# Macaron block on one core: all nine second products of a group as split products, and a ninth low half made on GpSimd

## Chip, core and metric

The kernel runs on one NeuronCore of a Trainium2 chip. The metric is the device time of one execution in microseconds (us). Times are the median of three executions. All inputs and outputs are float32. The engines are called PE (TensorE), DVE (VectorE), ACT (ScalarE), POOL (GpSimd) and SP (SyncE, which here only issues DMAs).

## What is computed

```python
x = x + 0.5 * ffn(layernorm(x))        # x: 8 x 1024 x 128
x = x + attention(layernorm(x))        # causal, one head, width 128
x = x + 0.5 * ffn(layernorm(x))

def ffn(h):                            # h: tokens x 128
    cw = route(sigmoid(h @ Wg.T))      # 16 experts, 4 chosen per token, weights
    hid = relu(h @ W1[e].T) ** 2       # 64 wide per expert
    y = hid @ W2[e].T
    return sum_e(cw[e] * y[e]) + relu(h @ Ws1.T) ** 2 @ Ws2.T
```

## The kernel before

The 8192 tokens are cut into 64 tiles of 128 and 16 groups of four tiles (512 tokens). A feed-forward phase runs over the 16 groups, then attention runs over eight batches, then a second feed-forward phase runs over the same groups. That is 32 groups in all. Everything in a group is transposed: features lie on partitions, tokens on the free axis, so a PE product has 512 columns.

All 16 experts are computed for every token. Two experts of 64 make one chunk of 128 hidden features, eight chunks hold the experts and a ninth (index 8) the shared expert. So `NCH` is 9, and a group has nine first products (`up`) and nine second products (`down`), which add up in one PSUM bank.

Float32 accuracy comes from splitting. An operand is stored as a high half, rounded to the type fp32r, and a low half, the rest. `split3` (L1186) makes one product out of three fp32r matmuls: high by high, high by low, low by high. One of the second products, chunk 5 (`WHOLE = (5,)`, L121), is different: it is one plain float32 matmul on unsplit operands (L1249), which the profile shows as two passes.

For chunk m the work goes through the engines in this order:
- PE: `up` (L1237), three matmuls into one of three PSUM banks (`HB`).
- DVE: `gate` (L931), relu times the routing weight out of `wb` into `s_sb` (L939; L941 for the shared chunk).
- ACT: `square` (L499), the square of `s_sb` twice, once rounded into `g_hi` (L504, left out for chunk 5) and once in full into `g_f` (L505). The second one counts up `sq_done`.
- POOL: `lo_part` (L374), `g_lo = g_f - g_hi` (L379), which counts up `glo_done`. For chunk 5 it returns at once.
- PE: `down` (L1244). It waits for `glo_done`, or for `sq_done` where the chunk is 5.

In the trace `g_f` is called `shared`, and `g_hi` and `g_lo` are both called `shared_r`.

The order on each engine is written out by hand, and each engine runs its list in order. The bodies are L1314 (PE), L1013 (DVE), L557 (ACT) and L418 (POOL); two groups make one pass of the loop. The up product, gate, square and low half of a chunk stand `AHEAD` = 4 chunks ahead of its down product, and `s_sb`, `g_f`, `g_hi` and `g_lo` are rings of six. In between, every group also has on PE the router's product (L1227) and three sets of transposes (L1219, L1235, L1261); on DVE the routing (`route`, parts 0 to 9) and layer norm statistics; on ACT four normalisations (L460) and several copies; on POOL one power operation for both inverse roots, `inv_and_norm_root` (L391, the instruction is L398), and the low half of the next input, `x_lo_part` (L382, L385).

Where they stand on POOL within a group: low half of chunk 4, then at place c = 1 the power operation, which waits among others for `wsum_done` of DVE (L919); then the low halves of chunks 6, 7, 8 and of the next group's chunk 0; then `x_lo_part`; then the next group's 1, 2, 3 and 4. On DVE at place c = 0 stands route part 7, which ends with L914 (`chosen`, from two operands in SBUF); at c = 1 the gate of chunk 5 and route part 8, which ends with L919; at c = 2 the gate of chunk 6.

The routing weights of a group come as a broadcast over DMA: ACT copies them (`wT_copy`), SP stores them to DRAM and loads them spread over the partitions into `wb` (L318).

At the end of the first phase the attention's opening is woven into the last group (`begin`, L623 on ACT and L1098 on DVE): after the square of chunk 5 ACT copies `z_hi` (L593), and DVE makes `z_lo` from it (L1059) between the gates of chunks 6 and 7.

Of the kernel before, what the change touches and what calls it, by code (L numbers as in the profile page):

```python
# [26 lines left out]
ACT = mybir.ActivationFunctionType  # L27
AX = mybir.AxisListType

P = 128  # L30
# [73 lines left out]
def macaron_kernel(nc, x, Qw, Kw, Vw, Wg, bias_corr, W1, W2, Ws1, Ws2, out):  # L104
    B, S, D = x.shape
# [5 lines left out]
    F = E * I + Ws1.shape[0]  # L111
    NCH = F // P
# [5 lines left out]
    HB = 3  # L118
    RING = 6

    WHOLE = (5,)  # L121
    PREP = 4
    PR = 4
    PADT = 3 * TG
# [8 lines left out]
    with ExitStack() as ctx:  # L133
        def sb(name, shape, dt=F32):
            return ctx.enter_context(nc.sbuf_tensor(name, shape, dt))
# [12 lines left out]
        w1_lo = sb("w1_lo", [P, NCH, P], F32R)  # L148
        w2_hi = sb("w2_hi", [P, NCH, D], F32R)
        w2_lo = sb("w2_lo", [P, NCH, D], F32R)  # L150
        w2_f = sb("w2_f", [P, len(WHOLE), D])
        wgT = sb("wgT", [P, E])
        qkT = sb("qkT", [P, 2, P])
        m_hi = sb("m_hi", [P, P], F32R)
# [43 lines left out]
        s_sb = sb("s_sb", [P, RING, GT])  # L198
# [3 lines left out]
        g_f = shared[:, 0:RING * GT].rearrange("p (r n) -> p r n", r=RING)  # L202
        g_hi = shared_r[:, 0:RING * GT].rearrange("p (r n) -> p r n", r=RING)
# [22 lines left out]
        o_ps = [psum[:, 3, :], psum[:, 4, :]]  # L226
# [116 lines left out]
        @block.gpsimd  # L343
        def _(pool):
            nc.gpsimd.memset(ident[:], 0.0).then_inc(self_done, 1)
            nc.gpsimd.memset(maskb[:], 0.0).then_inc(self_done, 1)
            nc.gpsimd.memset(neg_half[:], -0.5).then_inc(const_done, 1)
            pool.wait_ge(self_done, 2)
            nc.gpsimd.affine_select(out=ident[:], in_=ident[:], compare_op=ALU.not_equal, fill=1.0, base=0,
                                    pattern=[[-1, P]], channel_multiplier=1).then_inc(const_done, 1)  # L350

            nc.gpsimd.affine_select(out=maskb[:], in_=maskb[:], compare_op=ALU.is_ge, fill=MASKED, base=0,
                                    pattern=[[-1, P]], channel_multiplier=1).then_inc(const_done, 1)

            nc.gpsimd.memset(x_sb[:, NT:NT + PADT, :], 0.0).then_inc(const_done, 1)

            def inv_std(S_, n, var, out_, readers):

                pool.wait_ge(S_.var_done, n + 1)
                for r, count in readers:  # L360
                    wait(pool, r, count)
                nc.gpsimd.tensor_tensor(out_, var, neg_half[:, 0:out_.shape[1]], ALU.pow).then_inc(S_.rstd_done, 1)  # L362

            def attention_inv(b):
                inv_std(AT, b, a_mv[:, :, 1], a_rstd[:], [(AT.zn_done, 2 * b)])

            def ffn(F):
                def norm_root(g):

                    pool.wait_ge(F.wsum_done, g + 1)  # L370
                    wait(pool, F.scw_done, g)
                    nc.gpsimd.tensor_tensor(wroot, wsum, neg_half[:, 0:TG], ALU.pow).then_inc(F.norm_done, 1)

                def lo_part(m, j):  # L374

                    if j % NCH in WHOLE:
                        return
                    pool.wait_ge(F.sq_done, m + 1)
                    nc.gpsimd.tensor_tensor(g_lo[:, j % RING, :], g_f[:, j % RING, :], g_hi[:, j % RING, :].bitcast(F32),  # L379
                                            ALU.subtract).then_inc(F.glo_done, 1)  # L380

                def x_lo_part(g, u):  # L382

                    pool.wait_ge(F.xhi_done, g + 1)
                    nc.gpsimd.tensor_tensor(x_lo[:, u, :], x_f[:, u, :], x_hi[:, u, :].bitcast(F32),  # L385
                                            ALU.subtract).then_inc(F.xlo_done, 1)

                def inv(n):
                    inv_std(F, n, var, rstd, [(F.xn_done, n), (F.xn2_done, n)])

                def inv_and_norm_root(g):  # L391

                    pool.wait_ge(F.var_done, g + PREP + 1)
                    pool.wait_ge(F.wsum_done, g + 3)
                    pool.wait_ge(F.xn_done, g + PREP)
                    pool.wait_ge(F.xn2_done, g + PREP)
                    pool.wait_ge(F.scw_done, g + 2)
                    nc.gpsimd.tensor_tensor(roots[:], powers[:], neg_half[:, 0:2 * TG], ALU.pow).then_inc(F.rstd_done, 1)  # L398

                def start():  # L400
                    inv(0)
                    inv(1)
                    if F is FF[0]:
                        x_lo_part(0, 0)
                        norm_root(0)
                        inv(2)
                    else:
                        attention_inv(B - 1)
                        inv(2)
                        x_lo_part(0, 0)  # L410
                        norm_root(0)
                    x_lo_part(1, 1)
                    inv(3)
                    norm_root(1)
                    for m in range(AHEAD):
                        lo_part(m, m)

                def body(i, last):  # L418
                    for u in range(UN):
                        g = i * UN + u  # L420
                        for c in range(NCH):
                            j = u * NCH + c
                            if c == 1 and not last:
                                inv_and_norm_root(g)
                            if c == 6 and not last:
                                x_lo_part(g + 2, u)
                            if last and F is FF[0] and j == 4:
                                attention_inv(0)
                            if not (last and j + AHEAD >= UN * NCH):
                                lo_part(i * (UN * NCH) + j + AHEAD, (j + AHEAD) % (UN * NCH))  # L430

                start()
                body(0, False)
                with pool.Fori(1, NG // UN - 1) as i:
                    body(i, False)
                body(NG // UN - 1, True)

            ffn(FF[0])
            with pool.Fori(1, B - 1) as b:
                attention_inv(b)  # L440
            ffn(FF[1])
# [3 lines left out]
        def _(sc):  # L445
            copy = lambda o, i, scale=1.0: nc.scalar.activation(o, i, ACT.Copy, scale=scale)  # L446
# [20 lines left out]
            def ffn(F, phase):  # L467
# [31 lines left out]
                def square(m, j):  # L499

                    sc.wait_ge(F.s_done, m + 1)
                    wait(sc, F.down_done, m + 1 - RING)
                    if j % NCH not in WHOLE:
                        nc.scalar.activation(g_hi[:, j % RING, :], s_sb[:, j % RING, :], ACT.Square)  # L504
                    nc.scalar.activation(g_f[:, j % RING, :], s_sb[:, j % RING, :], ACT.Square).then_inc(F.sq_done, 1)  # L505

                def first_half(n):
# [46 lines left out]
                def lead(c):  # L554
                    square(c, c)
# [122 lines left out]
            def weights_hi(w):  # L678

                sc.wait_ge(wt_done, w + 1)  # L680
                src = wt_ps[w]
                flat = lambda a, k: a[:, 4 * k:4 * k + 4, :].rearrange("p c n -> p (c n)")
                if w < 2:
                    copy(flat(w1_hi, w), src).then_inc(wt_hi, 1)
                elif w < 4:
                    for n, c in enumerate(WHOLE):
                        if c // 4 == w - 2:
                            copy(w2_f[:, n, :], src[:, (c % 4) * P:(c % 4 + 1) * P])
                    copy(flat(w2_hi, w - 2), src).then_inc(wt_hi, 1)
                else:  # L690
                    copy(w1_hi[:, NC, :], src[:, 0:P])
                    copy(w2_hi[:, NC, :], src[:, P:2 * P])
                    copy(qkT[:].rearrange("p c n -> p (c n)"), src[:, 2 * P:4 * P]).then_inc(wt_hi, 1)
# [489 lines left out]
        def _(pe):  # L1183
            mm = nc.tensor.matmul
# [29 lines left out]
            def ffn(F, phase):  # L1214
# [29 lines left out]
                def down(g, c, m, j, u):  # L1244
                    if c == 0:
                        wait(pe, F.oT_copied, g - 1)
                    if c in WHOLE:
                        pe.wait_ge(F.sq_done, m + 1)
                        mm(o_ps[u], w2_f[:, WHOLE.index(c), :], g_f[:, j % RING, :], start=(c == 0),  # L1249
                           stop=(c == NCH - 1)).then_inc(F.down_done, 1)  # L1250
                        return
                    pe.wait_ge(F.glo_done, g * (NCH - len(WHOLE)) + sum(k not in WHOLE for k in range(c + 1)))
                    split3(o_ps[u], w2_hi[:, c, :], w2_lo[:, c, :], g_hi[:, j % RING, :], g_lo[:, j % RING, :],
                           start=(c == 0), stop=(c == NCH - 1)).then_inc(F.down_done, 1)

# [268 lines left out]
```

## Time and profile before

| | |
|---|---|
| median of 3 executions | 702.88 us (702.61 to 703.27) |
| the profiled execution's own time | 702.95 us |
| its span, first to last instruction | 701.2 us |
| PE busy | 673.3 us (96%) |
| DVE busy | 567.5 us (81%) |
| ACT busy | 529.6 us (76%) |
| POOL busy | 438.2 us (62%) |
| first feed-forward phase | about 33 to 268 us |
| attention | about 268 to 466 us |
| second feed-forward phase | about 466 to 701 us |

Busy shares are means over stages: POOL has next to nothing to do in attention, so its 62% says little of its load in the two other phases. The granted PE clock is at its full level (2.4 GHz, shown as 1.0) in the whole span. Matmul ends in the records are modelled, so the distance from one start to the next tells more of what a matmul costs than its duration.

### The profile page before, as it was taken

To read this page: it belongs to the slowest core of one execution; us is meant where nothing else is said; L and a number is where in the kernel's file an instruction comes from. 1 tells how busy PE (TensorE), PEld (TensorE's weight loads), DVE (VectorE), ACT (ScalarE), POOL (GpSimd) and SP (SyncE) were. 2 spreads that over 40 slices of the span, in tenths; PEclk is the share of its full clock that TensorE was granted. 3 is DMA by queue.
4 is the path that set the end of the run, shared out by engine and by line. 5 is a ranking of instruction groups with operands and counts; after the bars stand their busy time and mean duration, and the time that the engine had idled before them with its cause. 6 is when DMAs were issued, how large, how long until landed. Compare 5 with 4: busy or idle time off the path is not lost.

```text
span 701.2 us, 15091 instructions
## 1 busy us (share of the span) xinstructions
PE 673.3 (96%) x3367; PEld 527.5 (75%) x3367; DVE 567.5 (81%) x2586; ACT 529.6 (76%) x1094; POOL 438.2 (62%) x346
## 2 busy tenths in 40 slices
PE   4799999999999997999999999999999999999997
PEld 4567878888788875787778777778788887888775
DVE  5898998899888985666656678898988998889863
ACT  3578888888888866675566477659888788887875
POOL 3379888998889972000000021148889898898875
PEclk9999999999999999999999999999999999999999
DMA  9856776567765640000000000365776787767782
GB/s 246 196 124 138 162 165 145 124 147 154 162 143 123 152 90 0 1 1 1 0 1 0 0 0 1 71 134 115 158 166 140 166 179 171 165 139 174 166 178 72
DMA packets 53525, 78.37 MB, mean 112 GB/s; under 512 B 5216, under 2 KB 19184, under 8 KB 53488
## 3 DMA queue, kind: packets, MB, share of 16 engines
q1 hardware_dynamic: 51280, 77.36, 50.4%
q10 hardware_dynamic: 2208, 0.59, 0.4%
q8 instruction: 14, 0.23, 0.1%
q14 instruction: 23, 0.19, 0.1%
HBM read 72.70 MB, written 5.24 MB: 111 GB/s over the span
## 4 chain that ended last, share of the span: by engine, by line
PE 78%; DVE 10%; ACT 5%; issue 3%; POOL 1%; DMA 1%; POOLq 0%; DVEq 0%; ACTq 0%
PE psum L1188 18%; PE psum L1190 18%; PE psum L1189 18%; PE psum L1397 7%; PE psum L1227 4%; PE psum L1249 4%; DVE nmax L1068 3%; PE psum L1219 2%; PE psum L1261 2%; PE psum L1386 2%; ACT shared L611 2%; PE psum L1410 2%; DVE zn L1082 1%; DVE s_sb L939 1%; ACT wb L446 1%
## 5 line engine op out<-in xcount | busy, mean ns | idle before, releaser
L379 POOL TENSOR_TENSOR shared_r<-shared,shared_r 128x512 fp32r<-128x512 f32 x256 | 325.9, 1294 | 55.6 <-ACT shared L505 53.5
L939 DVE SCALAR_TENSOR_TENSOR s_sb<-psum,wb 128x512 f32<-128x512 f32 x256 | 175.5, 687 | 46.2 <-PE psum L1190 25.9
L505 ACT ACTIVATE shared<-s_sb 128x512 f32<-128x512 f32 x288 | 178.1, 620 | 28.6 <-DVE s_sb L939 28.6
L504 ACT ACTIVATE shared_r<-s_sb 128x512 fp32r<-128x512 f32 x256 | 159.8, 624 | 45.3 <-DVE s_sb L939 43.5
L1188 PE MATMUL psum<-x_hi,w_hi 128*128 128x512 f32 x288 | 127.2, 442 | 1.0 <-DVE x_sb L1094 0.5
L1190 PE MATMUL psum<-x_hi,w_lo 128*128 128x512 f32 x288 | 114.3, 397 | 0.0
L1189 PE MATMUL psum<-x_lo,w_hi 128*128 128x512 f32 x288 | 113.5, 394 | 0.0
L1188 PE MATMUL psum<-shared_r,w_hi 128*128 128x512 f32 x256 | 109.5, 428 | 0.8 <-POOL shared_r L379 0.7
L1189 PE MATMUL psum<-shared_r,w_hi 128*128 128x512 f32 x256 | 101.2, 395 | 0.0
L1190 PE MATMUL psum<-shared_r,w_lo 128*128 128x512 f32 x256 | 101.0, 395 | 0.0
L362 POOL TENSOR_TENSOR a_rstd<-a_mv,neg_half 128x8 f32<-128x8 f32 x8 | 13.1, 1636 | 116.4 <-DVE a_mv L758 116.4
L1188 PEld LDWEIGHTS psum<-x_hi,w_hi 128*128 128x128 f32 x288 | 54.5, 189 | 21.6 <-issue 7.2
L1189 PEld LDWEIGHTS psum<-x_lo,w_hi 128*128 128x128 f32 x288 | 54.4, 189 | 18.1 <-issue 7.2
L611 ACT ACTIVATE shared<-psum,nmax 128x128 f32<-128x128 f32 (+3 forms) x64 | 47.5, 742 | 23.5 <-DVE nmax L1068 22.2
L1190 PEld LDWEIGHTS psum<-x_hi,w_lo 128*128 128x128 f32 x288 | 54.2, 188 | 12.9
L1068 DVE TENSOR_REDUCE nmax<-psum 128x1 f32<-128x128 f32 (+3 forms) x64 | 47.5, 751 | 19.8 <-PE psum L1377 19.6
L1188 PEld LDWEIGHTS psum<-shared_r,w_hi 128*128 128x128 f32 x256 | 48.2, 188 | 13.6 <-POOL shared_r L379 3.8
L460 ACT ACTIVATE xn<-x_sb,shift,roots 128x128 f32 (+1 forms) x128 | 55.5, 481 | 2.7 <-DVE shift L778 2.7
L1190 PEld LDWEIGHTS psum<-shared_r,w_lo 128*128 128x128 f32 x256 | 48.1, 188 | 11.3
L1189 PEld LDWEIGHTS psum<-shared_r,w_hi 128*128 128x128 f32 x256 | 48.5, 189 | 7.7 <-issue 0.2
L398 POOL TENSOR_TENSOR roots<-powers,neg_half 128x8 f32<-128x8 f32 x28 | 45.8, 1637 | 9.2 <-DVE powers L919 5.5
L1397 PE MATMUL psum<-wb,zn 128*128 128x512 f32 (+3 forms) x128 | 47.2, 513 | 0.0
(166 smaller groups left out, 1301.5 us busy)
## 6 DMA issues: line engine op xcount, KB each, us to landing
wb<-scratch SPq DMA_DIRECT2D x128, 512.0 KB, 8.3
out<-x_sb SPq DMA_DIRECT2D x16, 256.0 KB, 9.8
x_sb<-in_L_attn_x SPq DMA_DIRECT2D x4, 256.0 KB, 6.1
scratch<-wT SPq DMA_DIRECT2D x32, 32.0 KB, 1.9
w_raw<-in_L_ffn_W ACTq DMA_DIRECT2D x1, 512.0 KB, 5.8
w_raw<-in_L_ffn_W SPq DMA_DIRECT2D x1, 512.0 KB, 6.7
w_raw<-in_L_ffn_Ws ACTq DMA_DIRECT2D x1, 64.0 KB, 8.6
w_raw<-in_L_ffn_Ws SPq DMA_DIRECT2D x1, 64.0 KB, 7.2
```

Of the source, the lines that this page charges most:

```text
L379: nc.gpsimd.tensor_tensor(g_lo[:, j % RING, :], g_f[:, j % RING, :], g_hi[:, j % RING, :].bitcast(F32), ALU.subtract).then_inc(F.glo_done, 1)
L398: nc.gpsimd.tensor_tensor(roots[:], powers[:], neg_half[:, 0:2 * TG], ALU.pow).then_inc(F.rstd_done, 1)
L460: ins = nc.scalar.activation(xn[:, t, :], x_sb[:, bass.ds(g * TG + t, 1), :].rearrange("p t d -> p (t d)"), ACT.Identity, bias=shift[:, t: ...
L504: nc.scalar.activation(g_hi[:, j % RING, :], s_sb[:, j % RING, :], ACT.Square)
L505: nc.scalar.activation(g_f[:, j % RING, :], s_sb[:, j % RING, :], ACT.Square).then_inc(F.sq_done, 1)
L611: nc.scalar.activation(prob[:, t % PR, 0:w], sc_ps[t % 2][:, 0:w], ACT.Exp, bias=nmax[:, u, t:t + 1], accum_out=rsum[:, u, t:t + 1]).then_ ...
L939: ins = nc.vector.scalar_tensor_tensor(s_, h_, 0.0, wb[:, u, c, :], ALU.max, ALU.mult)
L1068: nc.vector.tensor_reduce(nmax[:, u, t:t + 1], sc_ps[t % 2][:, 0:(t + 1) * P], AX.X, ALU.max, negate=True).then_inc(A.max_done, 1)
L1188: mm(out_, l_hi, r_hi, start=start, stop=False)
L1189: mm(out_, l_hi, r_lo, start=False, stop=False)
L1190: return mm(out_, l_lo, r_hi, start=False, stop=stop)
L1397: ins = mm(u_ps[:, q0:], zn[:, u, k, :], pT[half][:, k, q0:], start=(k == 0), stop=(k == last - 1))
```

## The change

Chunk 5 is treated as the eight others. ACT makes a high half for it too, POOL a low half, and PE three split matmuls in place of the whole one. The second product of chunk 5 then waits for POOL (`glo_done`) and no longer for ACT (`sq_done`). The unsplit weight `w2_f` and its copy in the opening go. The diff, whole:

```diff
@@ -118,7 +118,6 @@
-    WHOLE = (5,)
@@ -148,7 +147,6 @@
-        w2_f = sb("w2_f", [P, len(WHOLE), D])
@@ -373,8 +371,6 @@
                 def lo_part(m, j):
-                    if j % NCH in WHOLE:
-                        return
                     pool.wait_ge(F.sq_done, m + 1)
@@ -500,8 +496,7 @@
                     wait(sc, F.down_done, m + 1 - RING)
-                    if j % NCH not in WHOLE:
-                        nc.scalar.activation(g_hi[:, j % RING, :], s_sb[:, j % RING, :], ACT.Square)
+                    nc.scalar.activation(g_hi[:, j % RING, :], s_sb[:, j % RING, :], ACT.Square)
@@ -683,9 +678,6 @@
                 elif w < 4:
-                    for n, c in enumerate(WHOLE):
-                        if c // 4 == w - 2:
-                            copy(w2_f[:, n, :], src[:, (c % 4) * P:(c % 4 + 1) * P])
                     copy(flat(w2_hi, w - 2), src).then_inc(wt_hi, 1)
@@ -1244,12 +1236,7 @@
                 def down(g, c, m, j, u):
                     if c == 0:
                         wait(pe, F.oT_copied, g - 1)
-                    if c in WHOLE:
-                        pe.wait_ge(F.sq_done, m + 1)
-                        mm(o_ps[u], w2_f[:, WHOLE.index(c), :], g_f[:, j % RING, :], start=(c == 0),
-                           stop=(c == NCH - 1)).then_inc(F.down_done, 1)
-                        return
-                    pe.wait_ge(F.glo_done, g * (NCH - len(WHOLE)) + sum(k not in WHOLE for k in range(c + 1)))
+                    pe.wait_ge(F.glo_done, m + 1)
                     split3(o_ps[u], w2_hi[:, c, :], w2_lo[:, c, :], g_hi[:, j % RING, :], g_lo[:, j % RING, :],
                            start=(c == 0), stop=(c == NCH - 1)).then_inc(F.down_done, 1)
```

## Rows read from the trace of the kernel before

**Rows 1.** The page: busy time of each engine; shares of the chain that ended last.
```profile
PE 673.3 (96%) x3367; PEld 527.5 (75%) x3367; DVE 567.5 (81%) x2586; ACT 529.6 (76%) x1094; POOL 438.2 (62%) x346
...
PE 78%; DVE 10%; ACT 5%; issue 3%; POOL 1%; DMA 1%; POOLq 0%; DVEq 0%; ACTq 0%
```

**Rows 2.** Two steady groups: PE, PEld, DVE, ACT, POOL busy; clock, DMA share, GB/s.
```profile
140.19:169.28 29.09, 29.09 (x142) 23.39 (x141) 26.17 (x129) 25.07 (x53) 26.04 (x21) 1.00 0.67 146
```

**Rows 3.** Chain that ended last, a steady group: start, time on the chain, what.
```profile
140.00 0.23 PE psum L1188
...
141.40 0.23 PE psum L1188
...
147.56 0.86 PE psum L1249 x2
```

**Rows 4.** Timeline of POOL, a steady group: start, length, instruction, [idle before, releaser].
```profile
138.53 5.04 POOL L379 TENSOR_TENSOR shared_r<-shared,shared_r 128x512 fp32r<-128x512 f32 x4
143.87 1.64 POOL L398 TENSOR_TENSOR roots<-powers,neg_half 128x8 f32<-128x8 f32 x1 [0.30 <-issue]
145.69 2.55 POOL L379 TENSOR_TENSOR shared_r<-shared,shared_r 128x512 fp32r<-128x512 f32 x2 [0.19 <-ACT shared L505]
148.70 1.29 POOL L379 TENSOR_TENSOR shared_r<-shared,shared_r 128x512 fp32r<-128x512 f32 x1 [0.46 <-ACT shared L505]
150.52 1.29 POOL L379 TENSOR_TENSOR shared_r<-shared,shared_r 128x512 fp32r<-128x512 f32 x1 [0.52 <-ACT shared L505]
...
153.03 5.04 POOL L379 TENSOR_TENSOR shared_r<-shared,shared_r 128x512 fp32r<-128x512 f32 x4
158.53 1.64 POOL L398 TENSOR_TENSOR roots<-powers,neg_half 128x8 f32<-128x8 f32 x1 [0.46 <-DVE powers L919]
```

**Rows 5.** Timeline of POOL, second phase, a power operation with no idle before it.
```profile
487.86 1.63 POOL L398 TENSOR_TENSOR roots<-powers,neg_half 128x8 f32<-128x8 f32 x1
```

**Rows 6.** Timeline of DVE: L914 in two groups that follow each other.
```profile
141.23 1.19 DVE L914 SCALAR_TENSOR_TENSOR chosen<-marked,scores 128x64 f32<-128x64 f32 x1
...
156.25 0.67 DVE L914 SCALAR_TENSOR_TENSOR chosen<-marked,scores 128x64 f32<-128x64 f32 x1
```

**Rows 7.** Timeline of ACT: first square of chunk 6 in a steady group.
```profile
144.46 0.63 ACT L504 ACTIVATE shared_r<-s_sb 128x512 fp32r<-128x512 f32 x1 [0.78 <-DVE s_sb L939]
```

**Rows 8.** Timeline of PE: second products of chunk 5 and of the next chunk 1.
```profile
147.39 1.02 PE L1249 MATMUL psum<-shared,w_f 128*128 128x512 f32 x2
...
155.09 0.40 PE L1188 MATMUL psum<-shared_r,w_hi 128*128 128x512 f32 x1
```

**Rows 9.** Timelines of POOL and of PE in the first group of all.
```profile
42.72 1.64 POOL L398 TENSOR_TENSOR roots<-powers,neg_half 128x8 f32<-128x8 f32 x1
...
44.19 1.02 PE L1249 MATMUL psum<-shared,w_f 128*128 128x512 f32 x2
...
48.26 0.63 PE L1219 MATMUL psum<-ident,xn 128*128 128x128 f32 x4 [0.82 <-ACT xn L460]
```

**Rows 10.** Timelines of ACT, DVE and PE at the end of the first phase.
```profile
260.05 0.63 ACT L505 ACTIVATE shared<-s_sb 128x512 f32<-128x512 f32 x1 [0.55 <-DVE s_sb L939]
...
261.20 0.69 DVE L1059 TENSOR_TENSOR z_lo<-psum,z_hi 128x512 fp32r<-128x512 f32 x1
...
266.34 0.50 PE L1188 MATMUL psum<-shared_r,w_hi 128*128 128x512 f32 x1 [0.28 <-POOL shared_r L379]
```

**Rows 11.** Timelines of DVE, POOL and PE in the last group of all.
```profile
682.34 1.89 DVE L939 SCALAR_TENSOR_TENSOR s_sb<-psum,wb 128x512 f32<-128x512 f32 x3 [2.76 <-DMA wb<-scratch]
...
684.29 6.32 POOL L379 TENSOR_TENSOR shared_r<-shared,shared_r 128x512 fp32r<-128x512 f32 x5 [2.17 <-ACT shared L505]
690.79 1.29 POOL L379 TENSOR_TENSOR shared_r<-shared,shared_r 128x512 fp32r<-128x512 f32 x1 [0.18 <-ACT shared L505]
692.63 2.68 POOL L379 TENSOR_TENSOR shared_r<-shared,shared_r 128x512 fp32r<-128x512 f32 x2 [0.54 <-ACT shared L505]
...
695.36 0.50 PE L1188 MATMUL psum<-shared_r,w_hi 128*128 128x512 f32 x1 [0.38 <-POOL shared_r L379]
```

## Prediction, made before the changed kernel was run

> **What bounds the kernel now.** The page's busy line gives PE 96% of the span, and the chain that ended last is 78% PE [rows 1]. The means hide the stages, so the next view is the busy time of each engine over two steady groups: PE is busy for all 29.09 us, DVE for 26.17, ACT for 25.07 and POOL for 26.04 [rows 2]. Per group that is 14.55 us for PE and 13.02 for POOL. So 28 or so of the 32 groups go at PE's pace, but POOL, which looks idle on the page (62%), has only 1.5 us left in a group. The chain through a steady group is matmul after matmul with no wait in it [rows 3]. What PE saves there comes off the span, as long as POOL, which gets the work, keeps up.
>
> **What PE saves.** In the chain six split matmuls take from 140.00 to 141.40, 0.233 us each, so a split product of three costs 0.70 us. The whole product of chunk 5 stands there with 0.86 us for its two passes [rows 3]. The difference is 0.16 us; as the rounding hides up to 0.01, I take 0.155. Over 32 groups that is 5.0 us if nothing else moves. PE's period would go from 14.55 to 14.39 us.
>
> **What POOL gets.** Four low halves back to back take 5.04 us, the last one with its modelled 1.29, so one costs (5.04 - 1.29) / 3 = 1.25 us, and I take 1.255 [rows 4]. The group's POOL list becomes nine low halves, one x low half of the same shape, and the power operation at 1.62: 10 x 1.255 + 1.62 = 14.17 us against a period of 14.39. The new item stands right after the power operation. Walked through the steady group [rows 4]: power operation 143.87 to 145.50; chunk 5 to 146.75; chunk 6 to 148.0 (before 146.95); 7 to 149.3 (148.2); 8 to 150.5 (150.0); then the next chunk 0 would start at 150.5, and it started at 150.52 before. The idle stretches of 0.19, 0.46 and 0.52 us take up nearly all of the 1.25. The power operation has no idle before it where POOL is behind [rows 5], so nothing there costs time by itself.
>
> **Who waits for that.** The new wait of PE is for the low half of chunk 5, and queued behind it on PE is everything else. It would be ready at 146.75, and PE gets there at 147.39: 0.64 us to spare. For chunk 1 of the next group, made at about 154.28, PE comes at 155.09 [rows 8]: 0.8 to spare. PE's lead over POOL may so grow by about 0.5 us before it stalls. On ACT the extra square costs its pitch of some 0.53 us and stands before the square of chunk 6, ahead of which ACT idles 0.78 us [rows 7]: hidden in steady groups. Where that cover is gone, it costs up to 0.53 (below). DVE and the queue of SP get nothing new. The opening's copy of the unsplit weight is worth 0 to 0.2 us; I take 0, since the waits behind it are on other work.
>
> **A second loop at the same pace.** DVE's L914 takes 1.19 and 0.67 us in two groups that follow each other [rows 6], for 64 elements. It ends at 142.42 and 156.92, just behind an end of a POOL low half: 138.53 + 3 x 1.255 = 142.30 and 153.03 + 3.765 = 156.80 [rows 4]. So DVE is held until POOL's running instruction ends. The Trainium skill ("SBUF — State Buffer", section "Who interferes with whom") has this as a rule: a DVE instruction with two SBUF inputs and a GpSimd one that reads SBUF exclude each other for the whole instruction; the trace agrees, with 1.19 us. Behind L914 come L919 and the gate of chunk 6, then ACT's run of squares, then POOL's chunk 0, and with it the three low halves that end L914's next wait. This loop takes 14.50 us (142.42 to 156.92); as two groups take 29.09 [rows 2], the next round takes 14.59. On average that is what PE takes. It can only go faster if L914 arrives before the low half ahead of it ends: 141.05 against its arrival at 141.23. PE needs to lead by 0.18 us for that, and then L914 is let go a whole 1.25 us earlier. I expect that: once PE is ahead, L914 comes early in every other group, the pair takes 14.17 + 14.59 = 28.76 us, and PE at 28.78 is the pace again.
>
> **The edges.** First group: the power operation runs from 42.72 to 44.34 [rows 9], the low half of chunk 5 then to 45.6, and PE wants it at 44.19. It stalls 1.5 us, but had a wait of 0.82 us on ACT at 48.26 plus some 0.3 of slack in reading it; following the products up to there leaves +0.16 us where a saving of 0.155 stood. Bounds: -0.155 and +0.6.
>
> End of the first phase: ACT's second square of chunk 5 starts at 260.05 after an idle wait for DVE, right behind it comes the copy of z high, and DVE's z low starts at 261.20 [rows 10], when that copy ends. One more square in front moves it by 0.53. Behind z low stand the gates of chunks 7 and 8, and the last second product waits for POOL at 266.34. Price +0.52; bounds 0 and 0.53. The savings of the last two groups are lost too, as PE waits there anyway.
>
> Last group: its gates wait 2.76 us for the DMA of the routing weights, POOL 2.17 us after it [rows 11], so what PE saves in the group before is lost. From 684.29 POOL makes five low halves, up to 690.6; now chunk 5 to 691.9, 6 to 693.1, 7 to 694.4, 8 to 695.65. Chunk 8 ended at 692.63 + 2.68 = 695.31, and the last product waited for it [rows 11]. Price +0.36; bounds 0.3 and 0.6.
>
> **Sum.** First phase: +0.16, 13 groups by -0.155 = -2.0, then +0.52: -1.35. Second phase: 14 groups by -0.155 = -2.2, then +0.36: -1.8. Together -3.15 us, from the profiled execution's 702.95 (span 701.2) to 699.8. The median stands 0.07 below that execution, so 699.7 for the median.
>
> **Rivals.**
> Lock-step (0.14): L914 is not let go early, the DVE, ACT and POOL loop keeps its 14.55 us per group and PE idles 0.155 in each. For it speaks that the loop has no gap of its own now; against it that 0.18 us of lead suffices. Only the edges remain: 0.16 + 0.52 + 0.36 = +1.0, so 703.9. The rule of the Trainium skill named above speaks for this rival: more POOL time, more blocked DVE.
>
> POOL as the bound (0.12), the one on the slower side: POOL's idle of 0.30 before the power operation [rows 4] (0.46 in the next group) is tied to L919 and remains, while the rest is filled. A group then takes 14.17 + 0.46 = 14.63 us, or +0.08 over 27 groups = 2.2, plus the edges 1.0: 706.1. If the 0.19 behind the power operation stays as well, it is 14.82 and some 711. It decides as soon as POOL's group passes 14.55. Against it: rows 5, where that idle is zero.
>
> All of it (0.12): the edges cost nothing and the last groups give their part, -5.0: 697.9.
>
> Forecast as above: 0.62, from 698.8 to 701.3 by the bounds of the edges and by a steady saving between 0.10 and 0.16.
>
> **How the numbers follow.** A measurement of this kernel tells about 0.2% (1.4 us) from no change. Faster by more than that (under 701.5): forecast 0.60 of its 0.62 and the full saving 0.12, so 0.72. Within: lock-step 0.14 and the rest 0.02, so 0.16. Slower (over 704.3): 0.12. The range from 697.7 to 704.2 takes in all but the slower rival.
>
> **What would show it.** L1249 is gone and PE's period in steady groups is 14.39 us. POOL is busy for about 14.2 of it, and its waits for ACT before chunks 8 and 0 have shrunk to almost nothing. L914 takes about 0.2 us in some groups. PE's waits for L379 rise in the first group of all (1.5 us) and at the ends of both phases; z low moves by 0.5 us. A period of 14.55 with small PE waits in each group would mean lock-step; above 14.6 with PE waiting for L379 in every group, POOL as the bound. A slower clock than 1.00 would upset all of it.

## The result, and the profile after

The changed kernel took 709.69 us (median of four executions; 708.59 to 712.19) beside 703.08 us of the kernel before (702.61 to 703.68) on the same chip: a ratio of 1.0095, with an interval from 1.0072 to 1.0119. The forecast was 699.7 with a range up to 704.2, so it missed the time, the sign and the range. A second set of executions beside other runs gave 710.69 us and 1.0106 [1.0081, 1.0131]. The scatter grew as well: of the kernel before, 17 executions lay between 702.28 and 705.58; of the changed one, six lay between 706.5 and 713.13.

The profiled execution of the changed kernel took 708.59 us, with a span of 706.8. The page's busy line and the shares of the chain that ended last:

```profile
PE 672.9 (95%) x3399; PEld 531.4 (75%) x3399; DVE 575.2 (81%) x2586; ACT 546.9 (77%) x1125; POOL 475.5 (67%) x378
...
PE 52%; DVE 15%; issue 11%; DMA 7%; ACT 6%; POOL 6%; DVEq 1%; SPq 0%; POOLq 0%; ACTq 0%
```

Beside [rows 1], 78% of the chain was PE and now 52% is; what it lost went to "issue" (time in which an engine waits for nothing that the profile shows), to DMA, DVE and POOL. PE's busy time is hardly smaller, as a busy PE is counted up to a modelled end; the loss shows in the distance from group to group. Taken from one copy of oT (a group's output, still transposed) on ACT to the next, it was 14.50 and 14.60 us in turn before. Now the busy time of three stretches between such copies (us; busy PE, PEld, DVE, ACT, POOL; clock, DMA share, GB/s) reads:

```profile
127.82:143.72 15.90, 14.88 (x73) 11.91 (x72) 14.94 (x73) 13.05 (x28) 14.13 (x12) 1.00 0.65 134
143.72:158.04 14.32, 14.32 (x72) 11.81 (x71) 12.09 (x59) 13.17 (x28) 14.18 (x12) 1.00 0.68 149
172.74:201.64 28.90, 28.90 (x143) 23.61 (x142) 25.77 (x130) 26.24 (x55) 28.36 (x23) 1.00 0.70 147
```

The first line is one group of 15.90 us, in which PE and POOL both have holes; the second is the group right behind it. The third is a pair with no long group, 28.90 us beside the 29.09 of [rows 2] and the 28.76 that was forecast. The granted clock is 1.00 in all three, so it isn't the clock. What differs inside them is one instruction, L906 (L914 before). Timelines of DVE and of POOL in the long group, the start of DVE's L906 first:

```profile
129.04 2.23 DVE L906 SCALAR_TENSOR_TENSOR chosen<-marked,scores 128x64 f32<-128x64 f32 x1
131.19 0.68 DVE L931 SCALAR_TENSOR_TENSOR s_sb<-psum,wb 128x512 f32<-128x512 f32 x1
...
132.42 0.16 DVE L911 TENSOR_SCALAR powers<-psum 128x4 f32<-128x4 f32 x1
```

```profile
126.14 5.05 POOL L375 TENSOR_TENSOR shared_r<-shared,shared_r 128x512 fp32r<-128x512 f32 x4
132.96 1.64 POOL L394 TENSOR_TENSOR roots<-powers,neg_half 128x8 f32<-128x8 f32 x1 [1.77 <-DVE powers L911]
134.56 6.28 POOL L375 TENSOR_TENSOR shared_r<-shared,shared_r 128x512 fp32r<-128x512 f32 x5
140.79 1.32 POOL L381 TENSOR_TENSOR x_lo<-x_f,x_hi 128x512 fp32r<-128x512 f32 x1
```

L906 starts at 129.04, while the third low half of the run of four is on POOL. That one ends at 126.14 + 3 x 1.255 = 129.9, and L906 is not let in. It ends at 131.27, just behind the end of the whole run (131.19). Behind it are the gate L931, which had its input, and L911, for which POOL waits 1.77 us; behind POOL's power operation stand nine low halves with no gap, and PE waits 1.02 us for the first of them:

```profile
135.89 0.50 PE L1180 MATMUL psum<-shared_r,w_hi 128*128 128x512 f32 x1 [1.02 <-POOL shared_r L375]
```

Two groups further on the same instruction meets such a run of four in the same place, and is let in at the first end (156.39 + 3 x 1.255 = 160.2):

```profile
159.20 1.06 DVE L906 SCALAR_TENSOR_TENSOR chosen<-marked,scores 128x64 f32<-128x64 f32 x1
```

Five of the 32 took 2.2 us or more (2.98, 2.75, 2.23, 2.27 and 2.25), and each stands next to a distance of 15.69 to 15.92 us, in which POOL is idle for 1.5 to 1.8 us before the power operation. In the trace of before, none took over 1.21. All five end within 0.1 us of the end of POOL's run of low halves, when POOL has nothing left that it could start; the two longest had let two ends go by, the other three one. What the group loses is nearly the same: 15.69 and 15.73 us with two ends missed, 15.85 to 15.92 with one. By stretches, from the profiled executions: the first phase's 15 distances take 218.38 us instead of 213.94, the middle 217.74 instead of 217.18, the second phase's 15 take 212.48 instead of 211.83. With the 53.41 and 53.37 ahead of them this is all of the span's +5.6.

### The profile page after: what moved, and what is told of

Same layout as the page of the kernel before. It is cut to its first block, busy times and chain, and to the rows that moved or that the text cites. A ratio compares the mean times of both kernels' runs of the same rounds, so it can differ in the third digit from the quotient of the medians.

```text
span 706.8 us, 15086 instructions
## 1 busy us (share of the span) xinstructions
PE 672.9 (95%) x3399; PEld 531.4 (75%) x3399; DVE 575.2 (81%) x2586; ACT 546.9 (77%) x1125; POOL 475.5 (67%) x378
## 4 chain that ended last, share of the span: by engine, by line
PE 52%; DVE 15%; issue 11%; DMA 7%; ACT 6%; POOL 6%; DVEq 1%; SPq 0%; POOLq 0%; ACTq 0%
PE psum L1180 12%; PE psum L1182 11%; PE psum L1181 11%; PE psum L1384 7%; DMA wb<-scratch 5%; POOL shared_r L375 5%; DVE nmax L1060 3%; PE psum L1219 2%; DVE s_sb L931 2%; PE psum L1373 2%; ACT shared L606 2%; PE psum L1397 2%; PE psum L1211 2%; DVE zn L1074 1%; PE psum L1248 1%
## 5 line engine op out<-in xcount | busy, mean ns | idle before, releaser
L375 POOL TENSOR_TENSOR shared_r<-shared,shared_r 128x512 fp32r<-128x512 f32 x288 | 364.6, 1300 | 20.2 <-ACT shared L500 19.8
L499 ACT ACTIVATE shared_r<-s_sb 128x512 fp32r<-128x512 f32 x288 | 180.2, 626 | 60.6 <-DVE s_sb L931 57.3
L931 DVE SCALAR_TENSOR_TENSOR s_sb<-psum,wb 128x512 f32<-128x512 f32 x256 | 175.5, 688 | 43.9 <-PE psum L1182 20.2
L1180 PE MATMUL psum<-shared_r,w_hi 128*128 128x512 f32 x288 | 123.6, 429 | 7.9 <-POOL shared_r L375 7.8
L1180 PE MATMUL psum<-x_hi,w_hi 128*128 128x512 f32 x288 | 115.4, 401 | 1.0 <-DVE x_sb L1086 0.5
L1181 PE MATMUL psum<-shared_r,w_hi 128*128 128x512 f32 x288 | 113.8, 395 | 0.0
L1182 PE MATMUL psum<-shared_r,w_lo 128*128 128x512 f32 x288 | 113.6, 394 | 0.0
L1180 PEld LDWEIGHTS psum<-shared_r,w_hi 128*128 128x128 f32 x288 | 54.1, 188 | 30.0 <-POOL shared_r L375 20.3
L1060 DVE TENSOR_REDUCE nmax<-psum 128x1 f32<-128x128 f32 (+3 forms) x64 | 47.5, 752 | 19.8 <-PE psum L1364 19.7
L1182 PEld LDWEIGHTS psum<-shared_r,w_lo 128*128 128x128 f32 x288 | 54.0, 188 | 12.7
L1181 PEld LDWEIGHTS psum<-shared_r,w_hi 128*128 128x128 f32 x288 | 54.5, 189 | 7.4
```

Source lines behind the costliest of these rows:

```text
L931: ins = nc.vector.scalar_tensor_tensor(s_, h_, 0.0, wb[:, u, c, :], ALU.max, ALU.mult)
L1060: nc.vector.tensor_reduce(nmax[:, u, t:t + 1], sc_ps[t % 2][:, 0:(t + 1) * P], AX.X, ALU.max, negate=True).then_inc(A.max_done, 1)
L1180: mm(out_, l_hi, r_hi, start=start, stop=False)
L1181: mm(out_, l_hi, r_lo, start=False, stop=False)
L1182: return mm(out_, l_lo, r_hi, start=False, stop=stop)
```

## The experiments

**Is L906 the cause?** Its two inputs `marked` and `scores` lie in SBUF. The first run puts `marked` into PSUM, and changes nothing else but the place of one small tile: the step ahead of L907 reads `root` from SBUF (`root_sb`) in exchange, so it too has one input of each kind. Cut:

```diff
-        marked = sb("marked", [P, TG, E + 4])
+        root_sb = sb("root_sb", [P, TG, E])
...
+                self.marked = per_tile(cut[10])
...
-                        do(nc.vector.scalar_tensor_tensor(chosen[:], marked[:, :, 0:E], PICKED, score, ALU.is_ge, ALU.mult))
+                        do(nc.vector.scalar_tensor_tensor(chosen[:], T.marked[:, :, 0:E], PICKED, score, ALU.is_ge, ALU.mult))
```

> The changed kernel, with DVE's last step of route part 7 (chosen, L914 in the kernel before) reading its first operand (marked) from PSUM and not from SBUF, at no extra instruction. Theory 'lock': the changed kernel lost its time where this instruction waits for POOL's low halves, now and then for two of them in a row. Then the instruction takes about 0.2 us everywhere in the steady groups, the groups take 14.39 us, and the time is about 699.5 us (699.0 to 700.5). Rival 'throughput': POOL's list of 14.17 us plus hand-overs is too long for the period; then groups stay at 14.6 us or above and the time above 706 us. Rival 'latency': PE waits for the low half of chunk 5 behind the power operation; then PE's waits for POOL stay at 15 us or more in total.

Measured: 699.06 us (698.43 to 699.35), ratio 0.9945 [0.9928, 0.9962]. Groups of DVE instructions (count, busy us, mean ns), L907 of this kernel, then L906 of the changed one and L914 of the one before:

```profile
L907 DVE SCALAR_TENSOR_TENSOR chosen<-psum,scores 128x64 f32<-128x64 f32 x29 | 6.2, 213 | 0.0
```

```profile
L906 DVE SCALAR_TENSOR_TENSOR chosen<-marked,scores 128x64 f32<-128x64 f32 x32 | 29.2, 913 | 0.0
```

```profile
L914 DVE SCALAR_TENSOR_TENSOR chosen<-marked,scores 128x64 f32<-128x64 f32 x32 | 23.9, 746 | 0.0
```

The same work takes 0.21 us when POOL can't hold it. (The other three of the 32 in this kernel have both inputs in SBUF, at a time when POOL is idle there, and take 0.22.) The distances are 14.20 and 14.57 us in turn, and the sum of the two, 28.77, is the forecast pair. So the second product's split, POOL's ninth low half and ACT's extra square together give what was forecast, once this one instruction is out of POOL's way. PE's waits for low halves are 2.6 us in all, where the changed kernel has 7.8, so the rival in which the new wait of PE by itself makes the loss falls too. POOL in this kernel is just as full as in the changed one (here its timeline in a steady group; the 0.29 us is the only wait of over 0.1 us in a pair):

```profile
144.12 6.38 POOL L376 TENSOR_TENSOR shared_r<-shared,shared_r 128x512 fp32r<-128x512 f32 x5
150.46 1.31 POOL L382 TENSOR_TENSOR x_lo<-x_f,x_hi 128x512 fp32r<-128x512 f32 x1
151.72 5.06 POOL L376 TENSOR_TENSOR shared_r<-shared,shared_r 128x512 fp32r<-128x512 f32 x4
156.83 1.64 POOL L395 TENSOR_TENSOR roots<-powers,neg_half 128x8 f32<-128x8 f32 x1
158.43 5.06 POOL L376 TENSOR_TENSOR shared_r<-shared,shared_r 128x512 fp32r<-128x512 f32 x4
163.78 1.29 POOL L376 TENSOR_TENSOR shared_r<-shared,shared_r 128x512 fp32r<-128x512 f32 x1 [0.29 <-ACT shared L501]
```

A POOL that is busy nearly all of the time is therefore no loss by itself. The same kernel once more:

> The changed kernel with the first operand of the chosen-scores instruction in PSUM, once more, beside the version with z's high copy moved. Expected again at 699.1, 698.4 to 699.6, and long forms of the instruction in no group; the last distance of the first phase 9.96 us. If the gain of the first run of it was an accident of that run, it lies nearer to the 703 of the kernel before.

Measured: 699.97 us (699.23 to 700.58), 0.9953 [0.9939, 0.9966]. That is 0.4 us above the range expected here; the rest held, with no long form and a last distance of 9.99 us.

**Does the move to PSUM help alone?** The same edit on the kernel before:

> The kernel before with L914's first operand in PSUM, as in e1. Lock: L914 takes 0.2 us, but in the kernel before the time between low halves let it in at the next one each time and PE set the pace at 14.55 us, so nothing is gained: 702.7 us, within 0.2%. If the kernel before was itself held by this wait (the loop through DVE, ACT and POOL), it gets faster, down to 701 us.

Measured: 702.67 us (702.35 to 703.5), 0.9995 [0.9987, 1.0004]. No gain: DVE waits less there, and PE's period stands. What e1 gained over the changed kernel is not a gain of its own that any kernel would have; it takes away a loss that this change brought.

**The parts one at a time.** First the extra square on ACT alone, whose result nobody reads:

```diff
-                    if j % NCH not in WHOLE:
+                    if True:
                         nc.scalar.activation(g_hi[:, j % RING, :], s_sb[:, j % RING, :], ACT.Square)
```

> The kernel before with only the extra high-half square of chunk 5 on ACT, which nobody uses. All theories: steady groups unchanged at 14.55 us, +0.5 us at the end of the first phase (z high later by one square), so 703.6 us. If ACT were short in steady groups: 32 x 0.53 = 17 us more.

Measured: 703.36 us, 1.0009 [1.0000, 1.0019]. The last distance of the first phase goes from 9.47 to 9.97 us, the edge that was forecast at 0.52.

Then the same and POOL's ninth low half, with PE still on the whole product:

```diff
-                    if j % NCH in WHOLE:
-                        return
                     pool.wait_ge(F.sq_done, m + 1)
...
-                    pe.wait_ge(F.glo_done, g * (NCH - len(WHOLE)) + sum(k not in WHOLE for k in range(c + 1)))
+                    pe.wait_ge(F.glo_done, m + 1)
```

> The kernel before, in which ACT makes the high half and POOL the low half of chunk 5 too, but PE still uses the whole product, so nobody uses these halves. Lock: L914 is held for more than 2 us in a few groups as in the changed kernel, each costs about 1.25 us; 705 to 709 us. Throughput: POOL's list is the same 14.17 us against a period of 14.55; slower only if hand-overs add 0.4 us per group, then 705 or more with POOL never idle. Latency: PE does not wait for the low half of chunk 5 here, so 703.6 us (0.5 more than before, from the extra square at the end of the first phase).

Measured: 707.65 us (704.4 to 710.61), 1.0084 [1.0055, 1.0113]. The traced execution is the shortest of them, 704.4, and it has one long L912 (DVE, then POOL behind it):

```profile
68.37 2.45 DVE L912 SCALAR_TENSOR_TENSOR chosen<-marked,scores 128x64 f32<-128x64 f32 x1
...
72.78 1.64 POOL L396 TENSOR_TENSOR roots<-powers,neg_half 128x8 f32<-128x8 f32 x1 [2.05 <-DVE powers L917]
```

Its distance is 16.16 us. So the loss appears with PE's work as it was before. That the executions up to 710.61 have more of them is likely, but no trace of one was taken.

Last, ACT's square (the same edit as above) and PE's split without POOL's ninth low half, so that the result lacks this low half:

```diff
-                        mm(o_ps[u], w2_f[:, WHOLE.index(c), :], g_f[:, j % RING, :], start=(c == 0),
-                           stop=(c == NCH - 1)).then_inc(F.down_done, 1)
+                        split3(o_ps[u], w2_hi[:, c, :], w2_lo[:, c, :], g_hi[:, j % RING, :], g_hi[:, j % RING, :],
+                               start=(c == 0), stop=(c == NCH - 1)).then_inc(F.down_done, 1)
```

> The kernel before, with the high half of chunk 5 made by ACT and its second product as three fp32r matmuls, but without the low half on POOL: the high half stands in for it, so the middle product of chunk 5 is left out and replaced by a second high by high one. POOL's work is as before. If the DVE, ACT and POOL loop has room once PE leads (my forecast): 28 groups by -0.155 and +0.52 at the end of the first phase, 699.2 us. If that loop sets 14.55 us whatever PE does ('lock-step'): 703.6 us.

Measured: 698.44 us (698.26 to 698.79), 0.9938 [0.9922, 0.9955]. Here the loop gave way as it was forecast to: L914 comes early in many groups,

```profile
169.09 0.22 DVE L914 SCALAR_TENSOR_TENSOR chosen<-marked,scores 128x64 f32<-128x64 f32 x1
```

and its longest is 1.38 us. The 12 distances of the first phase between its first and its last two average 14.42, where the kernel before has 14.57. So PE's saving is there to be had (-4.2 us against the kernel before, 0.8 more than expected), and what is lost came in with POOL's part. The two don't simply add: -0.0062 and +0.0084 make 1.0022, and the whole change is at 1.0095 and 1.0106.

**Once more the changed kernel,** to see whether the long instructions are a habit or an accident of one trace:

> The changed kernel as it is, for its spread. Lock: the time depends on how often L914 misses an end of a low half, about 1.25 us each, so single executions differ by several times 1.25 us: from 704 to 712 us, median 708 to 710, where the kernels without that wait stay within 1 us.

Measured: 710.69 us. Eight of the 32 are long (2.18 to 3.01 us), in part in other groups than the first time; among them the one that had been let in at the first end in the other trace (159.20 there). All eight again end with POOL's run of low halves:

```profile
158.85 2.30 DVE L906 SCALAR_TENSOR_TENSOR chosen<-marked,scores 128x64 f32<-128x64 f32 x1
...
162.84 1.64 POOL L394 TENSOR_TENSOR roots<-powers,neg_half 128x8 f32<-128x8 f32 x1 [1.78 <-DVE powers L911]
```

**The price of one more end.** On the kernel before, with room on POOL, an instruction like L914 is put ahead of it, into a tile `twin` that is not read:

```diff
+                        nc.vector.scalar_tensor_tensor(twin[:], marked[:, :, 0:E], PICKED, score, ALU.is_ge, ALU.mult)
                         do(nc.vector.scalar_tensor_tensor(chosen[:], marked[:, :, 0:E], PICKED, score, ALU.is_ge, ALU.mult))
```

> The kernel before with one more DVE instruction like L914 (two SBUF operands, 64 elements, into a tile nobody reads) right ahead of it in every group. Free of waits it costs 0.13 us of DVE, of which DVE has 1.4 us to spare per group: then 703 us. Lock: both are held until a low half ends. If the second slips in with the first, 703 to 704 us; if each needs an end of its own, the loop through DVE, ACT and POOL grows by 1.25 us per group, less what DVE has to spare: 715 to 740 us.

Measured: 716.91 us (715.8 to 718.46), 1.0205 [1.019, 1.022].

```profile
158.65 1.17 DVE L915 SCALAR_TENSOR_TENSOR twin<-marked,scores 128x64 f32<-128x64 f32 x1
159.75 1.32 DVE L916 SCALAR_TENSOR_TENSOR chosen<-marked,scores 128x64 f32<-128x64 f32 x1
```

The second one needs an end of its own: it takes 1.30 to 1.33 us in 26 of the 32 groups (the other six meet no low half), and above it ends at 161.07, 1.25 us, one low half's start-to-start, behind the end of the first at 159.82. The distances become 14.48 and 15.83 us in turn. So one end more costs about 1.2 us of the group in which DVE is late (15.83 beside the 14.60 of before), here too, where POOL has idle time. The control has both instructions with an operand in PSUM:

> The kernel before with the twin instruction (the same sum of chosen scores written a second time, into a tile that nobody reads), as in the run that gave 716.91, but with the first operand of both in PSUM, so that neither has two inputs in SBUF. If the 14 us there were waiting for ends of low halves on POOL, both instructions take about 0.2 us here and the kernel stays at 702.7 to 703.5 (28 more instructions of 0.2 us on an engine with room). If they were the price of one more DVE instruction in that place, whatever its operands, it stays near 717.

Measured: 703.55 us (703.15 to 704.38), 1.0008 [0.9999, 1.0017], with 0.215 us for each of the two. The 13.4 us between the two runs are waiting for POOL's ends and not the price of one more DVE instruction.

**The edge of the first phase.** In e1's kernel the copy of z high is put ahead of chunk 5's two squares:

```diff
+                            if j == 10:
+                                extra(j)
                             if not (last and j + AHEAD >= UN * NCH):
                                 square(i * (UN * NCH) + j + AHEAD, (j + AHEAD) % (UN * NCH))
-                            extra(j)
+                            if j != 10:
+                                extra(j)
```

> e1 with the copy of z high put ahead of the squares of chunk 5 in the last group of the first phase. If the edge is as I priced it (+0.52 us from the extra square ahead of that copy), the first phase ends about 0.5 us earlier than in e1: 698.5 us against its 699.06, and the distance from the last but one to the last oT copy of that phase is 9.4 to 9.5 us and not 9.96. If the edge has another cause, no change.

> The same kernel with z's high copy ahead of chunk 5's squares, once more, beside the one without the move. If the edge of the first phase is worth its 0.45 us in the total, 698.6 and the last distance of the first phase 9.51 us; if what it gives there is lost in the groups that follow, the two agree within 0.3 us or this one is later, and the first groups of the second phase are longer than their 14.4 in its trace.

Measured: 700.0 (698.05 to 700.64) and 699.0 us (698.43 to 700.45), where the kernel without the move had 699.06 and 699.97. DVE's z low, without and with it:

```profile
259.35 0.69 DVE L1052 TENSOR_TENSOR z_lo<-psum,z_hi 128x512 fp32r<-128x512 f32 x1 [0.51 <-ACT z_hi L443]
```

```profile
258.56 0.67 DVE L1055 TENSOR_TENSOR z_lo<-psum,z_hi 128x512 fp32r<-128x512 f32 x1
```

The wait is gone, and the last distance of the first phase is 9.50 and 9.52 instead of 9.96 and 9.99 us. In the total this can't be told from nothing: the two kernels differ as much from one set of executions to the other as from each other. The forecasts for the distance held; the totals came out 1.5 and 0.4 us above theirs (698.5 and 698.6).

**Why is an end missed?** One idea was that POOL's next low half follows without a gap. A memset of one column, with no input, was put ahead of the low halves of chunks 3 and 4 of the changed kernel:

```diff
+                    if j % NCH in (3, 4):
+                        nc.gpsimd.memset(gap[...], 0.0)
                     pool.wait_ge(F.sq_done, m + 1)
```

> The changed kernel with one more instruction on POOL, a memset of one column (128x1, no input), ahead of the low halves of chunks 3 and 4, so that at the ends which the chosen-scores instruction missed POOL doesn't go from one low half straight to the next. It adds two short instructions to POOL's list of every group, an estimated 0.05 to 0.15 us each, which makes the list 14.3 to 14.45 us long: by itself +0 to +2 us in the kernel. If the ends are missed because the next low half follows at once, no chosen-scores instruction takes over 1.4 us here, POOL's waits of 1.5 to 1.8 us for the power operation are gone, and the kernel is at 701 to 704. If the gap doesn't matter, 3 to 8 of them take 2.2 to 3.0 us as before and the kernel is at 709 to 713.

Measured: 705.82 us (701.32 to 707.64), 1.0029 [1.0012, 1.0047]: neither what the idea expected nor what its rival did. The memset widens the step between two low halves by about 0.02 us only, and long instructions are still there, four in the traced execution:

```profile
155.98 2.46 DVE L909 SCALAR_TENSOR_TENSOR chosen<-marked,scores 128x64 f32<-128x64 f32 x1
```

```profile
155.68 0.16 POOL L376 MEMSET gap<- 128x1 f32 x1
155.73 1.34 POOL L378 TENSOR_TENSOR shared_r<-shared,shared_r 128x512 fp32r<-128x512 f32 x1
156.95 0.16 POOL L376 MEMSET gap<- 128x1 f32 x1
157.00 1.35 POOL L378 TENSOR_TENSOR shared_r<-shared,shared_r 128x512 fp32r<-128x512 f32 x1
```

L909 misses the end at about 156.95 although a memset stands there, and is let in when the run is over, at about 158.35. So a memset doesn't open the door, but with 0.02 us more between two low halves it hardly made a gap either; what a real one does wasn't tried here. Why the kernel is 4 to 5 us faster than the changed one all the same was not found; four long instructions instead of five or eight may be a part of it. Not every long distance comes from them: the longest of this trace, 16.40 us, has L909 at 0.22 us, and in it a gate waits 3.3 us for the routing weights:

```profile
525.67 0.69 DVE L934 SCALAR_TENSOR_TENSOR s_sb<-psum,wb 128x512 f32<-128x512 f32 x1 [3.32 <-DMA wb<-scratch]
```

## Why the prediction was wrong, step by step

**PE's saving** held. With L907 out of the way (e1) a pair takes 28.77 us, 14.385 per group; the forecast was 14.39.

**POOL's list** held. Where POOL doesn't wait, its power operations follow each other at 14.11 us (132.96 to 147.07 in the changed kernel); the forecast was 14.17. The idle stretches for ACT were filled: POOL's waits for the squares fell from 53.5 us in all to these 19.8:

```profile
L375 POOL TENSOR_TENSOR shared_r<-shared,shared_r 128x512 fp32r<-128x512 f32 x288 | 364.6, 1300 | 20.2 <-ACT shared L500 19.8
```

**Who waits** held: PE's wait in the first group was 1.30 us where 1.5 was forecast, and that stretch ends at 53.37 instead of 53.41, 0.04 us earlier where 0.16 later was forecast; the 14 traces have it between 52.98 and 53.62, so neither can be told from nothing. The end of the first phase cost 9.98 - 9.47 = 0.51 (forecast 0.52), the last group 9.44 - 9.12 = 0.32 (forecast 0.36). The middle, forecast at nothing, took 0.56 us more; it was 0.32 to 0.54 in several of the other kernels too, e9 without any of the change among them, and has no explanation here. None of these is the step that failed: the terms forecast for the edges come out within 0.2 us each.

**The second loop** is the step that failed. Its first half was right: L906 does come early in every other group of a steady stretch (0.49 us at 114.16, 0.50 at 144.19, 0.47 at 173.25, 0.48 at 202.15; the prediction had it at about 0.2), the loop of DVE, ACT and POOL is not rigid, and pairs without a long instruction take 28.9 to 29.0 us, some 0.2 more than the forecast 28.76. But the prediction let L906 go at the next end of a low half at the latest, as in the trace of before. That is what doesn't hold: in the changed kernel it misses that end in 5 and in 8 of the 32 groups, and is then held until POOL's run of low halves is over, one or two ends later. It happens in both groups of a pair. In the second execution the one that asks early is held for 3.01 us (DVE, then POOL):

```profile
204.12 3.01 DVE L906 SCALAR_TENSOR_TENSOR chosen<-marked,scores 128x64 f32<-128x64 f32 x1
...
201.98 5.06 POOL L375 TENSOR_TENSOR shared_r<-shared,shared_r 128x512 fp32r<-128x512 f32 x4
208.58 1.64 POOL L394 TENSOR_TENSOR roots<-powers,neg_half 128x8 f32<-128x8 f32 x1 [1.53 <-issue]
```

What the prediction put at nothing is the price of such a group, 1.3 to 1.5 us over its 14.39, and POOL's idle time behind it. The sentence that carried it was "DVE is held until POOL's running instruction ends". The Trainium skill ("SBUF — State Buffer", section "Summary: rules for kernel authors") says of such a pair that the second one to issue is blocked until the first finishes. The trace of before agrees with that, these traces do so only in part, with 2.2 to 3.0 us where POOL's next instruction started 0.1 to 0.9 us after the request.

The size fits. In the first phase e1's 15 distances take 212.21 us and the changed kernel's 218.38, 6.2 more. Four of them hold a long instruction (15.69, 15.73, 15.90, 15.92); against 14.385 they are 5.7 us longer. In the second phase the difference is 2.8 us, of which the one long instruction, with a distance of 15.85, makes 1.5; the rest is about that of two distances of 14.99 and 15.32, in which DVE's gate waits 1.28 and 1.52 us for the routing weights (DMA). Such a wait isn't new: the trace of before has one of 1.54 us, in a distance of 15.40.

**The rivals.** Lock-step was wrong in its mechanism: the loop doesn't keep its old pace. "POOL as the bound" had the right place, POOL waiting for the power operation with a list that has no room left, and the wrong size: a wait of 0.46 us in every group, where the trace has none or 0.5 in most and 1.5 to 1.8 in a few. And a full POOL isn't a bound at 14.55, as e1 shows. The right rival would have been this: of two engines that lock each other out, one runs without a gap through the moment at which the other asks, and may keep the other out until its run is over; such a group costs 1.3 us or more, and two of them in a phase eat all that PE saves there (13 x 0.155 = 2.0 us). The prediction had the row for that price [rows 4] and the row for the lock [rows 6], and took the one outcome that was seen as the only one.

**What is open.** What decides whether an end is missed. In the traces it is not the moment of the request alone: at 0.30 us into a low half L906 was let in at the next end (159.20) or wasn't (158.85, the second execution), and 0.88 us into one it took 0.50 us (144.19) or 3.01 (204.12, the second execution). Nor is it POOL's run of four alone, which stands in the kernel before as well (138.53, 5.04 us [rows 4]). What the 18 long ones of four traces (5, 8, 4 and 1) have in common is how they end: with POOL's run, the four that missed two ends as well as the 14 that missed one. That a real gap in that run would let DVE in is likely from this, and not shown. That the long ones come with POOL's ninth low half is shown: none in the traces of before, e3, e4 and e8, one to eight in those of e2, e12 and the changed kernel. Of the one execution of before that took 705.58 us there is no trace.

## What to carry to other kernels

Before work is given to POOL, look in DVE's timeline for instructions with two inputs in SBUF that take longer than their like (here 0.67 and 1.19 us for what takes 0.21), and ask who is queued behind them. Such a wait is no constant: price it once with the next end of POOL's instructions and once with the end of their whole run, and put the dearer one into the range. Moving one input to PSUM is a cheap cure, worth nothing before the change (702.67 beside 702.79) and some 10 us after it; with it the change is a gain, 699.06 and 699.97 us instead of some 702.8.

## What the runs showed of the hardware

- A DVE instruction with both inputs in SBUF, 128x64, that takes 0.21 us with one input in PSUM, took 2.13 to 3.01 us beside POOL low halves of 1.255 us each: it was passed over at one or two of their ends. All 18 such cases ended within 0.1 us of the end of POOL's run; in four of them two ends were passed over before it. The same program did this in 5 groups in one execution and in 8 in another.
- Two such instructions in a row don't share an end: the second took 1.30 to 1.33 us in 26 of 32 groups (e8), so each of them costs one POOL instruction.
- A memset of 128x1 between two POOL instructions shows 0.09 to 0.17 us in the records, and opened no safe place for DVE (an instruction of 2.46 us missed the end with it); it widened the step between them by 0.02 us only.
